# Attention and a gated layer on one core: the maxima's pieces spread anew over the groups, and an earlier load of the output weights

## The chip, the cores and the metric

The kernel runs on one core of a Trainium2 chip. The metric is the time of one execution on the device in microseconds. TensorE is PE in the profile (its weight loads PEld), VectorE is DVE, ScalarE ACT, GpSimd POOL, SyncE SP; here SP issues nearly all DMAs, into one queue.

## The reference

```python
x = L0_attn_x                          # 2 x 1024 x 512
xn = _layernorm(x)
s = attention(xn, w_qkv, b_qkv, w_out, b_out)      # 32 heads of 16, ALiBi slopes, causal
g = _silu(ffn(xn, w_gate, w_up, w_down))           # silu(gate) * up, then down; hidden 1360
x = x + s * g
```

The three matrices of `ffn` are built from octonion blocks of ternary weights: each weight is rounded to -1, 0 or 1 times the mean size. The scores get a bias per head and key (ALiBi) and the causal mask before the softmax.

## The kernel before, in words

**Stages.** (1) In four chunks of 512 tokens: layer norm, x turned on PE, queries, keys and values as three-term f16 products, stored to HBM. Inside the same stretch the weights are turned and split, and the octonion matrices of the gated layer are made. (2) The gated layer, again in four chunks; each has 26 tiles (`ffn(j, p)`): 22 gate and up tiles in turn (an even tile is a gate tile: ACT takes its tanh, then DVE multiplies; an odd one is multiplied by DVE at once) and 4 tiles of the down product. (3) Attention in 16 groups of four heads (2 batches of 8). (4) The output product, gate and residual, partly beside the last group.

**A group.** `scores(t, n, pair)` makes a tile of transposed scores with the mask added, 10 steps by 2 pairs; ACT takes the exponential; `products(t, n)` multiplies it with the values, 10 steps, with 32 columns of the array for each head. The exponential needs each row's maximum. So a pass goes ahead of the group: `fill_max(t, i)` (line 1519) computes scores once more, untransposed, into one of **three** PSUM banks, and DVE's `read_max` takes the maxima (line 1237 plain, line 1233 with the mask added). A group of heads has 42 such pieces: 41 tiles and, as piece 5, a transposition (line 1512) by which the maxima of the group before become two rows of its queries' operand (`Qs`, the name is `QKs` in the profile). Piece numbers 13 to 28 are plain 512-wide reduces; the others are masked, 128 to 512 wide. `fill_max` waits until DVE has read the piece three before it:

```python
elif at >= MRING:
    pe.wait_ge(max_read, tiles_read(at - MRING))
```

**The order of work.** `ORDER` is one list of all pieces of stages 2 to 4, written by `work_order`, and every engine walks through it. Beside stage 2 it strews the first pieces of the maxima (`early`: all 41 tiles of group 0 and pieces 0 to 18 of group 1) between the tiles of the third and fourth chunk: after each tile it computes how many are due and puts them in when that is at least three. In stage 3, one string `GROUP` of 72 letters (M a piece of the maxima, S scores, P products) gives the order within each group: 42 M, of which the first finish the next group's maxima and the last 14 or so begin those of the group after next. So each group begins with the same pieces done ahead.

**Loads.** `load(t)` on SP brings queries, keys, slopes and values of group t into one of three slots, with 15 DMAs; it is issued for t + 2 at the start of group t, once all scores of group t - 1 are filled. The first piece of group t + 2's maxima waits for all of them.

**The first stage's queue.** `store_qkv(c)` stores a query or key tile each time one is ready, with the loads of the gated layer's weights (`load_gated`, lines 512 to 523) between those of chunk 0; as number 6 the output weights (`w_out`, 1 MB, into `wslot[3]`, a part of `room`). Then come the four value stores. `next_x` (line 539) loads the next chunk's x. DVE's `third` and `values` write into two stage buffers each and wait for the store of the tile two before. `LN_AT[c][stage]` says after which query or key tile DVE does the five stages of the next chunk's layer norm (statistics, their sums, variance, root, normalising), `ROOT_AT[c]` when ACT takes the square root.

## Time and profile before

| | us |
|---|---|
| median of 3 runs | 829.93 |
| lowest, highest | 829.28, 832.33 |
| the profiled execution | 828.85 |
| its span | 827.0 |
| PE busy in the span | 794.2 (96%) |
| DVE busy | 606.6 (73%) |
| ACT busy | 473.6 (57%) |
| POOL busy | 172.0 (21%) |

The busy shares are means over the stages; the rows further down take the stages apart. The end of a matmul is modelled, and matmuls overlap in the array: two that use different halves of its rows run side by side. A row of the timeline gives the start, the busy time, and in brackets how long the engine idled before it and for whom.

### The profile page before, as it was taken

To read this page: it belongs to the slowest core of one execution; us is meant where nothing else is said; L and a number is where in the kernel's file an instruction comes from. 1 tells how busy PE (TensorE), PEld (TensorE's weight loads), DVE (VectorE), ACT (ScalarE), POOL (GpSimd) and SP (SyncE) were. 2 spreads that over 40 slices of the span, in tenths; PEclk is the share of its full clock that TensorE was granted. 3 is DMA by queue.
4 is the path that set the end of the run, shared out by engine and by line. 5 is a ranking of instruction groups with operands and counts; after the bars stand their busy time and mean duration, and the time that the engine had idled before them with its cause. 6 is when DMAs were issued, how large, how long until landed. Compare 5 with 4: busy or idle time off the path is not lost.

```text
span 827.0 us, 16157 instructions
## 1 busy us (share of the span) xinstructions
PE 794.2 (96%) x5927; PEld 350.2 (42%) x5927; DVE 606.6 (73%) x1743; ACT 473.6 (57%) x633; POOL 172.0 (21%) x214
## 2 busy tenths in 40 slices
PE   5989999999999999999999999999999999999998
PEld 3545444444444444444444434344343334343333
DVE  6837888643232464464599999999999999996546
ACT  7424384332232222232688888888888788887540
POOL 3223222233434333333300000000000003530000
PEclk9999999999999999999999999999999999999999
DMA  7474422259202101101222122222215233642736
GB/s 267 143 214 158 141 102 77 104 139 302 90 1 89 65 1 39 63 2 39 77 68 66 57 60 73 81 80 68 81 53 168 69 106 104 199 152 101 229 127 221
DMA packets 71104, 88.40 MB, mean 107 GB/s; under 512 B 26898, under 2 KB 37150, under 8 KB 70512
## 3 DMA queue, kind: packets, MB, share of 16 engines
q1 hardware_dynamic: 70992, 87.36, 32.8%
q8 instruction: 47, 0.77, 0.4%
q14 instruction: 33, 0.27, 0.1%
q0 software_dynamic: 32, 0.01, 0.0%
HBM read 51.15 MB, written 35.93 MB: 105 GB/s over the span
## 4 chain that ended last, share of the span: by engine, by line
PE 73%; DVE 15%; DMA 5%; issue 4%; ACT 1%; POOL 1%; SPq 0%; DVEq 0%; ACTq 0%
PE psum L1562 13%; PE psum L1519 9%; PE psum L1585 9%; PE psum L1586 9%; DVE mx L1237 9%; PE psum L1596 5%; PE psum L1597 5%; PE psum L1537 4%; DVE mshown L1233 3%; PE psum L1411 3%; PE psum L1413 3%; PE psum L1412 3%; PE psum L1546 2%; PE psum L1621 1%; PE psum L1623 1%
## 5 line engine op out<-in xcount | busy, mean ns | idle before, releaser
L951 ACT ACTIVATE probs<-psum,exp_scale 128x1024 f32<-128x1024 f32 (+1 forms) x320 | 310.2, 1028 | 66.2 <-PE psum L1546 46.3
L1233 DVE CUSTOM_DVE_ANT_0 mshown<-psum,ahead 128x384 bf16<-128x384 f32 (+3 forms) x512 | 220.2, 487 | 2.7 <-PE psum L1519 0.4
L1519 PE MATMUL psum<-QKs 51*128 51x512 f16 (+3 forms) x768 | 183.6, 332 | 12.6 <-DVE mx L1237 6.3
L1562 PE MATMUL psum<-probs,Vs 128*32 128x512 f32 (+3 forms) x1536 | 162.0, 510 | 0.2 <-ACT probs L951 0.2
L1237 DVE TENSOR_REDUCE mx<-psum 128x1 f32<-128x512 f32 x256 | 157.7, 681 | 3.5 <-PE psum L1519 2.5
L1537 PE MATMUL psum<-QKs 53*128 53x512 f16 (+3 forms) x768 | 138.1, 330 | 3.1 <-ACT probs L951 3.0
L1585 PE MATMUL psum<-X,room 128*128 128x512 f16 (+1 forms) x352 | 133.6, 380 | 0.0
L1586 PE MATMUL psum<-X,room 128*128 128x512 f16 (+1 forms) x352 | 133.4, 379 | 0.0
L1519 PEld LDWEIGHTS psum<-QKs 51*128 51x128 f16 x768 | 51.6, 93 | 146.8 <-DVE mx L1233 74.8
L983 ACT ACTIVATE room<-psum,gate_half 128x512 f32<-128x512 f32 (+1 forms) x44 | 30.2, 687 | 101.4 <-PE psum L1586 101.4
L1260 DVE SCALAR_TENSOR_TENSOR room<-room,psum 128x512 f32<-128x512 f32 (+1 forms) x44 | 30.2, 687 | 63.1 <-ACT room L983 63.1
L811 POOL TENSOR_TENSOR room<-room 128x512 f16<-128x512 f32 (+1 forms) x44 | 50.9, 1156 | 114.3 <-ACT room L988 114.3
L785 POOL TENSOR_SCALAR mscaled<-mx 128x32 f32<-128x32 f32 x16 | 4.6, 289 | 314.6 <-DVE mx L1245 314.6
L1596 PE MATMUL psum<-room 128*128 128x512 f16 (+1 forms) x176 | 66.8, 379 | 0.0
L1597 PE MATMUL psum<-room 128*128 128x512 f16 (+1 forms) x176 | 66.6, 379 | 0.0
L1562 PEld LDWEIGHTS psum<-probs,Vs 128*32 128x32 f32 x1536 | 44.8, 145 | 44.3 <-issue 37.7
L775 POOL TENSOR_TENSOR qk_stage<-rest,qk_stage 128x512 f16<-128x512 f32 x32 | 37.9, 1185 | 105.1 <-DVE qk_stage L1161 105.1
L1546 PE MATMUL psum<-unit,causal 64*128 64x64 bf16 (+1 forms) x768 | 58.8, 200 | 0.0
L1537 PEld LDWEIGHTS psum<-QKs 53*128 53x128 f16 x768 | 45.2, 94 | 23.7 <-ACT probs L951 12.0
L1546 PEld LDWEIGHTS psum<-unit,causal 64*128 64x128 bf16 x768 | 49.3, 96 | 13.1 <-issue 0.7
L1269 DVE SCALAR_TENSOR_TENSOR room<-room,psum 128x512 f32<-128x512 f32 x16 | 11.0, 687 | 58.9 <-ACT room L983 58.9
L1585 PEld LDWEIGHTS psum<-X,room 128*128 128x128 f16 (+1 forms) x352 | 35.0, 99 | 44.3 <-issue 5.3
(166 smaller groups left out, 963.0 us busy)
## 6 DMA issues: line engine op xcount, KB each, us to landing
o_scr<-osum SPq DMA_DIRECT2D x32, 256.0 KB, 3.1
QKs<-q_scr SPq DMA_DIRECT2D x96, 64.0 KB
QKs<-k_scr SPq DMA_DIRECT2D x96, 64.0 KB
q_scr<-qk_stage SPq DMA_DIRECT2D x16, 256.0 KB, 2.6
k_scr<-qk_stage SPq DMA_DIRECT2D x16, 256.0 KB, 2.2
v_scr<-v_stage SPq DMA_DIRECT2D x16, 256.0 KB, 2.1
Vs<-v_scr SPq DMA_DIRECT2D x16, 256.0 KB
probs<-in_L_attn_x SPq DMA_DIRECT2D x4, 1024.0 KB, 11.0
```

Of the source, the lines that this page charges most:

```text
L811: nc.gpsimd.tensor_tensor(HLs[0:n, t, :], hid[t % NSIG][0:n], HHs[0:n, t, :], ALU.subtract).then_inc(hl_done, 1)
L951: nc.scalar.activation(probs[n % PSLOTS][:, 2 * pair:2 * pair + 2, 0:COLS[n]], s_bank[pair][:, :, 0:COLS[n]], ACT.Exp, scale=exp_scale[:, ...
L1233: last = nc.vector.tensor_tensor_reduce(out=mshown[tiles_read(at) % 2][:, cols], in0=m_bank[bank][:, cols], in1=ahead[:, CH - keys:], scal ...
L1237: nc.vector.tensor_reduce(dst, m_bank[bank][:, 0:n * keys].rearrange("p (n k) -> p n k", n=n), AX.X, ALU.max).then_inc(max_read, 1)
L1519: last = nc.tensor.matmul(tile[:, hh, :], Qs[s][rows, pair + hh, qb * P:(qb + 1) * P], Ks[s][rows, pair + hh, k0:k0 + keys], start=(hh == ...
L1537: last = nc.tensor.matmul(s_bank[pair][:, u, at:at + cols], Ks[s][rows, pair, kb * P:(kb + 1) * P], Qs[s][rows, pair, (c + 1) * CH - cols: ...
L1546: last = nc.tensor.matmul(squares, causal[half, r], unit[half, 0, 0:HALF].unsqueeze(1).to_broadcast([HALF, len(blocks), HALF]), start=Fals ...
L1562: last = nc.tensor.matmul(pv_bank[32 * h:32 * h + 32, CH - cols:CH], Vs[s][:, kb, h::QH], probs[n % PSLOTS][:, h, at:at + cols], start=(kb ...
L1585: nc.tensor.matmul(bank[0:n], wt, X16[j % 2][:, 0, kt, :], start=(kt == 0), stop=False)
L1586: last = nc.tensor.matmul(bank[0:n], wt, X16[j % 2][:, 1, kt, :], start=False, stop=(kt == KT - 1))
L1596: nc.tensor.matmul(bank, HHs[0:n, k, tok], MD[0:n, k, :], start=(k == 0), stop=False)
L1597: last = nc.tensor.matmul(bank, HLs[0:n, k, tok], MD[0:n, k, :], start=False, stop=(k == HT - 1))
```

## The change

Three parts.

**The maxima run further ahead, and come back piece by piece.** `AHEAD` says how many pieces of the group after next's maxima are done when group t begins: 25 at group 0, one less with each group, 11 from group 14 on. So groups 1 to 13 hold 41 pieces, and 74 instead of 60 stand beside the gated layer (67 by `line(0)`, 8 more by `OPENING`, less the piece that group 0 doesn't need). They are strewn by the same rule as before (at least three due), which now gives batches of three and of four.

**Each group has its own string.** `GROUPS` has 15, by `GROUP_AT`; the last is the old one and serves groups 14 and 15. Group 0 has 33 pieces, and its first tile of scores is put at its very start.

**The output weights** are issued in the first queue, behind the bias row and ahead of the second chunk's x. The second chunk's layer norm moves by one tile, the root too.

```diff
+GROUPS = [
+    "SMSPPMPMSMMSMMSMSMPSMMMSPMSMMPS"
+    "MMSMPMMSMPMMSSMPMSMSMMPMSMSMSMSM",
+    "MPMSMPMMSMSPMMMSSMMPMSMMSMPMSMMSMPM"
+    "MSMSMPMMSMMSMMPMMSMPMSSMMMPMSMSMMSSM",
...
+GROUP_AT = [0, 1, 2, 3, 4, 5, 6, 7, 8, 9, 10, 11, 12, 13, 14, 14]
+PER_GROUP = 41
 OPENING = 8
-GROUP = "MPMMPSMMSMPMMSSMMMSSMMPMSMMSPMMSMPMM" \
-        "SMSMMPMSMMMMSSMPMMSPMMSSMMPMMSMSMMSM"
+AHEAD = [LEAD + (QUADS - 2 - t) * (NITEM - PER_GROUP) for t in range(QUADS - 1)] + [LEAD]
+
+
+def line(t):
+
+    return (t + 1) * NITEM + AHEAD[t]
...
-    items = [(t + 1, i) for i in range(LEAD, NITEM)] + [(t + 2, i) for i in range(LEAD)]
+    items = [divmod(i, NITEM) for i in range(line(t) + OPENING * (t == 0), line(t + 1) if t < QUADS - 1 else line(t) + NITEM)]
...
-    for kind in GROUP:
+    for kind in GROUPS[GROUP_AT[t]]:
...
-    early = [(0, i) for i in range(NITEM) if i != ROWS_AT] + [(1, i) for i in range(LEAD + OPENING)]
+    early = [divmod(i, NITEM) for i in range(line(0) + OPENING) if i != ROWS_AT]
...
         if t == 0:
-            opening = [w for w in pieces if w[0] == "maximum"][:OPENING]
-            pieces = [w for w in pieces if w not in opening]
+            pieces.sort(key=lambda w: w != ("scores", 0, 0, 0))
...
-        LN_AT = [[1, 2, 2, 3, 4], [2, 3, 4, 5, 6], [1, 2, 2, 3, 4]]
-        ROOT_AT = [2, 4, 2]
+        LN_AT = [[2, 3, 3, 4, 5], [2, 3, 4, 5, 6], [1, 2, 2, 3, 4]]
+        ROOT_AT = [3, 4, 2]
...
-                elif m == 6:
-                    sp.dma_start(wslot[3], w_out.rearrange("(t p) d -> p t d", p=P)).then_inc(w_loaded[3], 16)
...
             sp.dma_start(bv_row[:], b_qkv[2 * D:3 * D].partition_broadcast(P)).then_inc(bv_loaded, 16)
+            sp.dma_start(wslot[3], w_out.rearrange("(t p) d -> p t d", p=P)).then_inc(w_loaded[3], 16)
             next_x(1)
```

**SP, the first chunk.** Before: the start of the queue, then its part around the output weights (`room<-in_L_attn_w_out`); a name in brackets is the semaphore waited for.

```order
L595 DMA bv_row<-in_L_attn_b_qkv 128x512
L539 DMA xin<-in_L_attn_x 128x4x512 [waits xt_done]
...
L521 DMA room<-in_L_ffn_w_down 64x8x170
L529 DMA k_scr<-qk_stage 128x2x512 [waits q3_done]
L523 DMA room<-in_L_attn_w_out 128x4x512
L529 DMA k_scr<-qk_stage 128x2x512 [waits q3_done]
L535 DMA v_scr<-v_stage 128x512 [waits evac_done] x4
```

Now:

```order
L630 DMA bv_row<-in_L_attn_b_qkv 128x512
L631 DMA room<-in_L_attn_w_out 128x4x512
L574 DMA xin<-in_L_attn_x 128x4x512 [waits xt_done]
...
L558 DMA room<-in_L_ffn_w_down 64x8x170
L564 DMA k_scr<-qk_stage 128x2x512 [waits q3_done] x2
L570 DMA v_scr<-v_stage 128x512 [waits evac_done] x4
```

The output weights went from between the last two key stores to ahead of the second load of `xin`, and the value stores (`v_scr`) have only stores ahead of them.

**PE, the gated layer.** Before, a batch of the fourth chunk between two gate or up tiles; the lines 1585 and 1586 are a gate or up tile, line 1519 pieces of the maxima.

```order
L1586 MATMUL psum<-X,room 80x512
L1519 MATMUL psum<-QKs 128x512 [waits max_read] x3
L1585 MATMUL psum<-X,room 80x512 [waits f_evac]
L1586 MATMUL psum<-X,room 80x512
L1585 MATMUL psum<-X,room 80x512
```

Now a batch after tile 14 of the fourth chunk (lines 1621, 1622 and 1555 in the new file):

```order
L1622 MATMUL psum<-X,room 128x512
L1555 MATMUL psum<-QKs 128x512 [waits max_read] x4
L1621 MATMUL psum<-X,room 128x512 [waits f_evac]
L1622 MATMUL psum<-X,room 128x512
L1621 MATMUL psum<-X,room 128x512
```

Where every batch had three pieces, six of the 23 now have four; each piece waits for a bank (`max_read`).

**PE, the first group of attention.** Before (L1537 scores, L1546 their mask, L1519 pieces of the maxima), from the second tile of scores on:

```order
L1537 MATMUL psum<-QKs 128x512 [waits exp_done,f_evac]
L1537 MATMUL psum<-QKs 128x512
L1546 MATMUL psum<-unit,causal 128x64 x4
L1537 MATMUL psum<-QKs 128x256 [waits exp_done]
L1537 MATMUL psum<-QKs 128x256
L1546 MATMUL psum<-unit,causal 128x64 x4
L1537 MATMUL psum<-QKs 128x256 [waits exp_done]
L1537 MATMUL psum<-QKs 128x256
L1546 MATMUL psum<-unit,causal 128x64 x4
L1519 MATMUL psum<-QKs 128x512 [waits max_read] x3
```

Now, from the end of the gated layer (L1573 scores, L1582 mask, L1555 pieces):

```order
L1555 MATMUL psum<-QKs 128x128 [waits max_read] x2
L1555 MATMUL psum<-QKs 128x256 [waits max_read]
L1555 MATMUL psum<-QKs 128x256
L1573 MATMUL psum<-QKs 128x512 [waits exp_done,m_stacked,f_evac]
L1573 MATMUL psum<-QKs 128x512
L1582 MATMUL psum<-unit,causal 128x64 x4
L1555 MATMUL psum<-QKs 128x256 [waits max_read]
L1555 MATMUL psum<-QKs 128x256
L1573 MATMUL psum<-QKs 128x512 [waits exp_done,f_evac]
L1573 MATMUL psum<-QKs 128x512
L1582 MATMUL psum<-unit,causal 128x64 x4
L1555 MATMUL psum<-QKs 128x384 [waits max_read] x2
```

Four tiles of scores stood together ahead of the first piece; now pieces stand between the first and the second, and between all that follow.

## Rows read from the trace of the kernel before

**Rows 1.** Stage windows: us; per engine busy (instructions); granted clock, DMA share, GB/s.
```profile
56.32:279.70 223.38, 223.27 (x1146) 106.09 (x1148) 118.19 (x242) 86.96 (x163) 74.26 (x62) 1.00 0.37 122
279.70:400.00 120.30, 120.30 (x575) 51.14 (x576) 64.15 (x165) 31.11 (x51) 43.90 (x39) 1.00 0.08 31
...
401.36:755.00 353.64, 339.74 (x3502) 140.51 (x3506) 347.00 (x1181) 300.29 (x337) 36.34 (x68) 0.99 0.31 91
```

**Rows 2.** Waits of the whole run: waiting line <- awaited line: us, times, longest.
```profile
PEld psum L1519 <- DVE mx L1233: 74.8, 153, 0.8
```

**Rows 3.** Window of one group of four heads.
```profile
448.06:471.98 23.92, 23.12 (x245) 9.57 (x246) 23.59 (x80) 20.47 (x23) 0.74 (x3) 1.00 0.24 67
```

**Rows 4.** Timeline, PE, 30 to 57 us: start, us, instruction, [idle before it <- releaser].
```profile
32.80 0.66 PE L1380 MATMUL psum<-identf,room 128*128 128x128 f32 x4 [0.89 <-DVE W L1065]
...
56.32 0.39 PE L1411 MATMUL psum<-X,W 128*128 128x512 f16 x1 [2.35 <-DVE X L1057]
```

**Rows 5.** Timeline, SyncE's DMA issues, 15 to 60 us.
```profile
15.21 0.37 SPq L539 DMA_DIRECT2D xin<-in_L_attn_x  x1
...
45.19 0.47 SPq L523 DMA_DIRECT2D room<-in_L_attn_w_out  x1
...
47.65 9.95 SPq L535 DMA_DIRECT2D v_scr<-v_stage  x4
```

**Rows 6.** Timeline, DVE, 15 to 60 us.
```profile
29.04 2.47 DVE L1029 BATCH_NORM_STATS2 stats<-xin 128x6 f32<-128x512 f32 x4
31.66 0.43 DVE L1161 CAST qk_stage<-rest 128x512 f16<-128x512 f32 x1
...
54.69 1.06 DVE L1166 TENSOR_TENSOR v_stage<-psum,bvs_row 128x512 f32<-128x512 f32 x1 [4.97 <-DMA v_scr<-v_stage]
```

**Rows 7.** DMA issues up to 90 us: what, count, KB each, median us to landing.
```profile
room<-in_L_attn_w_out SPq DMA_DIRECT2D x1, 1024.0 KB, 6.6
```

**Rows 8.** Timeline, PE, 296 to 304 us: around a batch of three maxima.
```profile
298.99 0.38 PE L1586 MATMUL psum<-X,room 128*128 128x512 f16 x1
...
299.83 0.39 PE L1585 MATMUL psum<-X,room 128*128 128x512 f16 x1
```

**Rows 9.** Timeline, DVE, in one group: sixteen plain reduces, one narrow masked one.
```profile
448.63 9.91 DVE L1237 TENSOR_REDUCE mx<-psum 128x1 f32<-128x512 f32 x16
458.45 0.28 DVE L1233 CUSTOM_DVE_ANT_0 mshown<-psum,ahead 128x128 bf16<-128x128 f32 x1
```

**Rows 10.** Timeline, DVE, gated layer: odd tile at 305.23, even at 311.77.
```profile
305.23 0.69 DVE L1256 SCALAR_TENSOR_TENSOR room<-psum,room 128x512 f32<-128x512 f32 x1 [0.32 <-PE psum L1586]
305.83 1.87 DVE L1237 TENSOR_REDUCE mx<-psum 128x1 f32<-128x512 f32 x3
...
311.77 0.69 DVE L1260 SCALAR_TENSOR_TENSOR room<-room,psum 128x512 f32<-128x512 f32 x1 [1.75 <-ACT room L983]
312.37 1.88 DVE L1237 TENSOR_REDUCE mx<-psum 128x1 f32<-128x512 f32 x3
```

**Rows 11.** Timeline, ACT, gated layer: the tanh of the same even tile.
```profile
311.05 0.69 ACT L983 ACTIVATE room<-psum,gate_half 128x512 f32<-128x512 f32 x1 [2.25 <-PE psum L1586]
```

**Rows 12.** Timeline, PE, one step of products.
```profile
459.75 1.09 PE L1562 MATMUL psum<-probs,Vs 128*32 128x512 f32 x8
```

**Rows 13.** Timeline, SyncE: first and last issue of a group's 15 loads.
```profile
446.12 0.79 SPq L553 DMA_DIRECT2D QKs<-q_scr  x2
...
452.59 0.52 SPq L561 DMA_DIRECT2D Vs<-v_scr  x1
```

**Rows 14.** Windows of 2 us: clock and DMA share.
```profile
54.00:56.00 2.00, 0.00 (x0) 0.00 (x0) 1.31 (x2) 0.00 (x0) 0.00 (x0) 1.00 0.02 9
400.00:402.00 2.00, 1.09 (x15) 0.56 (x15) 1.25 (x3) 1.84 (x3) 0.41 (x1) 1.00 0.34 131
404.00:406.00 2.00, 2.00 (x19) 1.25 (x15) 2.00 (x4) 1.19 (x2) 0.20 (x1) 0.50 0.37 134
456.00:458.00 2.00, 2.00 (x21) 0.78 (x24) 2.00 (x5) 2.00 (x3) 0.00 (x0) 1.00 0.03 8
```

More of the change, by code:

```diff
@@ L154, in tiles_read @@
     return at + 1 - rows_copied(at)
+GROUPS = [
[3 more added lines that the diff above has]
+    "MSMSMPMMSMMSMMPMMSMPMSSMMMPMSMSMMSSM",
+    "MPMSMMSPMSMMPMSMMSMMPMSMMSMPMMSSMMP"
+    "MMSMSMPMMSMSMMPMMMSPMMSMSMPMSMSMMSSM",
+    "MPMSMMSMPMSMPMMSMSMMMPMSMSMMPMSMMSP"
+    "MSMMSMMPMMSMSMMPMMSMSPMMSMPMMSMSSMSM",
+    "MPMSMPMMSSMMMSMPMMSMMSMPMMSMSMPMSMM"
+    "SMPMMSSMMPMMSMSMMPMMSMSMPMMSMSPMMSSM",
+    "MPMMSMSPMMMSMSMPMMSMSMMMPSMMSMPMSMM"
+    "SMPMMSMSMPMMSMSMMPMSMMSMPSMMMSPMSMMS",
+    "MPMSMSMPMSMMSMMSSMMPMMSMMSMPMSMPMSM"
+    "MPMSSMMPMSMMPMMSMMSMMSMMPMMSSMPMMSMS",
+    "MPMSMMMSPMSMMSMSSMMMPMSMMSMMPMSMPMM"
+    "SMPMSMSMPMSMMPMMSMSMMPMSMMPMSSMMMSMS",
+    "MPMSMSMMSMMMSSMSMMPSMMPMMSMSMMPMMPM"
+    "SMSMMPMSSMMPMMSMPMMSSMMMPMMSMSPMMSSM",
+    "MPMMSSMMPMSMSMSMMSMMSMSMPMMSMSMMPMS"
+    "MPMMSMPMMSSMPMSMMPMMSMSMMPMMMSPMMSSM",
+    "MPMSMSMMPSMMSMSMSMMMSMSMMPMMSMMSMPM"
+    "SMPMSMMPMMSMSPMMSMPMMSMSMMPMSMSMPMSM",
+    "MPMMSSMMMPSMMMSMSSMMPMSMSMMPMSMMSMM"
+    "MSMPMMSMPMSMSMPMSMMPMMSSMMMPSMMPSMSM",
+    "MPMSMSMPMMSMPMSMMSMPMSMSMPMSMMPMMSM"
+    "MSMPMMSSMMPMSMMSMPMMSSMMPMMSMMSMMSSM",
+    "MPMMSSMMPMSMPMSSMMMPMMSMSPMSMMPMSMM"
+    "MSMMPSMSMMPMSMMMSPMMSSMMPMMSMSMMSMSM",
+    "MPMMPSMMSMPMMSSMMMSSMMPMSMMSPMMSMPMM"
+    "SMSMMPMSMMMMSSMPMMSPMMSSMMPMMSMSMMSM",
+]
+GROUP_AT = [0, 1, 2, 3, 4, 5, 6, 7, 8, 9, 10, 11, 12, 13, 14, 14]
+PER_GROUP = 41
 OPENING = 8
-GROUP = "MPMMPSMMSMPMMSSMMMSSMMPMSMMSPMMSMPMM" \
-        "SMSMMPMSMMMMSSMPMMSPMMSSMMPMMSMSMMSM"
+AHEAD = [LEAD + (QUADS - 2 - t) * (NITEM - PER_GROUP) for t in range(QUADS - 1)] + [LEAD]
+def line(t):
+    return (t + 1) * NITEM + AHEAD[t]
 def group_order(t):
     scores = [(n, pair) for n in range(NST) for pair in range(2)]
-    items = [(t + 1, i) for i in range(LEAD, NITEM)] + [(t + 2, i) for i in range(LEAD)]
+    items = [divmod(i, NITEM) for i in range(line(t) + OPENING * (t == 0), line(t + 1) if t < QUADS - 1 else line(t) + NITEM)]
     products = [(t - 1, n) for n in range(NST - LAG, NST)] + [(t, n) for n in range(NST - LAG)]
     out = []
-    for kind in GROUP:
+    for kind in GROUPS[GROUP_AT[t]]:
         if kind == "S":
```

## Prediction

> **What bounds the kernel now.** I read the stage windows first: three stages and a tail. Up to 280 us and on to 400 us the tensor engine is busy all the time [rows 1]; that is where every microsecond of its work or idleness goes straight into the end. From 401.36 to 755 us DVE is busy 347.00 of 353.64 us [rows 1], and the page's waits show what that does to the tensor engine: its weight loads for the maxima wait 74.8 us in all for the masked reads of line 1233 alone [rows 2]. One group in this stage takes 23.92 us, of which DVE is busy 23.59, ACT 20.47 [rows 3]; the matmul column reads 23.12, but modelled ends hide short stops, and I take the tensor engine to have some 3 to 4 us of room a group. So the group stage is DVE's: shorten what DVE reads there and the stage shrinks, as long as the pieces can go where DVE has room. The gated stage has that room (DVE 64.15 of 120.30 us) but none on the tensor engine. After 755 us nothing changes. The rest of the idleness lies before 57 us: the tensor engine stops 2.35 us before the second chunk's first matmul and 0.89 us before a weight transposition [rows 4].
>
> Sum and rows are made against the profiled execution, 828.85 us (span 827.0), which stands 1.08 us under the median of 829.93.
>
> **1. Output weights earlier, layer norm one tile later.** Now the last 1 MB of weights is issued at 45.19 us, just ahead of the last key store and of the four value stores, issued from 47.65 us [rows 5]. DVE cannot write its third value tile before the first value store has landed: it idles 4.97 us and starts at 54.69 [rows 6], the split of x queued behind it ends after that, and the tensor engine's 2.35 us follow. With the weights gone from there the stores have 1 MB less ahead of them. DVE would have been free 4.97 us earlier, twice what the tensor engine waited, so the 2.35 us go wholly; next in line is the third value tile itself, which the tensor engine finishes before its last one. The weights now come between the projection weights and x of the second chunk, issued at 15.21 us and first read at 29.04 [rows 5, 6]: 13.8 us of slack against 6.6 us in which those weights landed in the busy place [rows 7]. That costs nothing. The 0.89 us come from DVE taking x's statistics (2.47 us at 29.04) ahead of the copy at 31.66 that lets the low weights go on [rows 4, 6]. Now the statistics stand one tile later. But each copy also needs an earlier store to have landed, and the normalising of x moves nearer to its transpositions at 44 us, so I take back about half: 0.5. Bounds: -3.2 us (both stops gone) and 0 (the stop only moves). I take **-2.9**.
>
> **2. Fourteen more pieces beside the gated layer, as matmuls.** There were 60 pieces (20 batches of three); the order now has 74 in 23 batches: one of two, sixteen of three, six of four. A batch of three 512-wide pieces takes the tensor engine from the slot after 298.99 (a slot there is 0.216 us, 299.205) to 299.83, so 0.62 us [rows 8], 0.21 a piece. Fourteen make 2.9, some of them narrow: **+2.7** (bounds 1.5, if the fourth of a batch runs beside the third on the other half of the rows, and 3.5).
>
> **3. The batches of four.** The maxima have three PSUM banks. The fourth piece of a batch fills the bank of the first, which DVE must have read; the tensor engine waits in order with the whole gated layer behind it. Never so before: all batches had three. How long it waits is in the trace. After an even gate tile (ends as ACT begins at 311.05) DVE first waits for the tanh, multiplies at 311.77 and reads its first maximum at 312.37; the read takes 0.62 us (16 in 9.91 us [rows 9]), so the bank is free 1.94 us after the tile's end [rows 10, 11]. The three fills take until about 0.36 us after it. The stop is 1.6 us. After an odd tile DVE multiplies at once (305.23) and reads at 305.83: free 1.22 us after the tile's end, a stop of 0.9 [rows 10]. Three of the six follow even tiles (14 of the third chunk, 2 and 14 of the fourth), three follow odd ones (21 of the third, 7 and 21 of the fourth): 3 x 1.6 + 3 x 0.9 = **+7.5**. The tensor engine has no other idle place to absorb it. Bounds: 4 (the next batch is already queued and DVE is early) and 9.
>
> **4. What DVE no longer reads after 401.36.** The pieces read after the last gated tile began with number 16 of the second group, now with number 30: numbers 16 to 28 are plain reduces, 13 x 0.62 = 8.06 us; number 29 is two masked 128-wide reads of 0.28 us that overlap a little [rows 9], about 0.45. **-8.5**. Each group after the first then has 41 pieces where it had 42, and lasts about 23.3 us instead of 23.92. ACT (20.47) still fits under that, and so does the tensor engine.
>
> **5. The orders by group.** The cover is now thinner: three engines between 88% (20.47 of 23.3) and 99%, three banks, and products that hold the tensor engine for 1.09 us [rows 12], in which three narrow pieces (0.28 us each) run out. DVE idles 6.6 us in the whole stage before the change. A different order in every group could save a tenth of a microsecond a group or lose three tenths. I take **+1.0** (bounds -2 and +4). The loads of the group after next must also land earlier, because its first piece comes after some 16 of the next group's instead of 28. They are issued from 446.12 to 452.59 us and the DMA engines are quiet from 456 on [rows 13, 14]: under 10 us; its first piece in the second group is filled about 9 to 10 us after the same point. So at most half a microsecond, once, and later groups have more. The number is in the +1.0.
>
> Sum: -2.9 + 2.7 + 7.5 - 8.5 + 1.0 = -0.2. 828.65 for the profiled execution, about 829.7 for the median; I say **829.5 us**. About 0.5% (4.1 us) is what a measurement of this kernel can tell from no change.
>
> **Rivals.**
> - *The stops of the fours don't come.* If DVE has always read the first bank when the fourth fill is due, part 3 is 1 to 3 us and the sum -5 to -7: 823 to 825. For it: DVE is busy only half of that stage. Against it: the reads start where the rows say, behind the tanh, and nothing can move them forward. With a group stage that comes out well (part 5 at -2) it also passes the 0.5%. Chance for faster on all such grounds 0.27.
> - *The clock falls at the new stops.* In the window 400 to 402 us the tensor engine was busy 1.09 of 2 us, and from 404 to 406 the granted clock is 0.50, the 1.2 GHz level instead of 2.4 [rows 14]. If that follows each of the six stops, then every time some 4 us of matmuls run at half speed in a stage that the tensor engine bounds: 2 us each, up to +12, so 834 to 842, slower. It decides as soon as three of the six do it. Against it: from 54 to 56 us the engine did nothing at all and the clock stayed at 1.00 [rows 14]; the two falls of the trace lie in the group stage, where matmuls use half the rows or 32 columns. The Trainium skill, "TensorE: Matmul & The Clock Gate", section "A second HAM failure mode: psum-queue depth-cycling", has it that short idle stops while PSUM banks are cycled can be enough to make the clock swing; by that rule this rival would be the likeliest and the time near 840. The trace agrees in the group stage and not at 54 us. Chance 0.13.
> - *The group stage loses its cover.* If each of fourteen groups idles 0.4 us more than now, part 5 is +6 and the time 835: slower. It is the point at which tensor engine work, not DVE reads, sets the group. Chance 0.10.
> - *The load does nothing.* If the value stores are slow for another reason than the weights, part 1 is 0 and the time 832.5: within 0.5%.
>
> **How the numbers follow.** Neutral 0.50, faster 0.27, slower 0.23 (the two slower rivals). The two parts that move most, 3 and 4, nearly cancel, and each is sized from rows; the neutral case's own range is 826 to 833. The overall range reaches to the favourable end of part 3 and to two or three clock falls or a loose group stage: 824 to 836.
>
> **What would show it.** The tensor engine busy without a stop from about 15 to 279 us except the small ones at the start, no wait at the second chunk; the value tile's wait for its store gone. In the gated stage (longer by 10 us, DVE busy some 8 us more) six new waits of the fills for DVE, 1.6 or 0.9 us. Read after that: 14 groups of about 23.3 us, DVE at 98%. Wrong would be: a gated stage longer by 3 us only (faster), granted clock under 1.00 in it (slower), groups still at 23.9 us (slower), or a wait for the loads at the start of the second group's pieces for the fourth.

## The result, and the profile after

| us | before | after |
|---|---|---|
| median (4 runs each) | 829.61 | 840.95 |
| lowest, highest | 826.9, 832.33 | 837.07, 842.26 |
| ratio to before | | 1.0134 (1.0106 to 1.0161) |
| the profiled execution, its span | 828.85, 827.0 | 839.78, 838.0 |

The changed kernel is slower by 1.3%, 11.3 us. I had forecast no change (829.5, range 824 to 836): wrong, and outside the range.

**Where the 11 us are.** The stage windows of the changed kernel stand against [rows 1]. To have the same borders in both kernels I cut at three events: the first gate tile, the first scores, and the last join of the partial maxima (`whole_rows`). In each row: its length; PE, PEld, DVE, ACT and POOL busy, with the number of instructions; granted clock, DMA share, GB/s. Before:

```profile
160.40:400.20 239.80, 239.80 (x1132) 105.77 (x1131) 102.80 (x221) 66.05 (x107) 89.59 (x77) 1.00 0.23 76
400.20:755.49 355.29, 341.12 (x3521) 141.13 (x3517) 348.06 (x1183) 301.82 (x339) 36.34 (x68) 0.99 0.31 92
```

After:

```profile
159.10:413.30 254.20, 246.68 (x1145) 107.06 (x1144) 111.48 (x238) 65.93 (x107) 89.67 (x77) 0.99 0.21 72
413.30:766.82 353.52, 339.52 (x3506) 138.19 (x3502) 339.86 (x1166) 303.36 (x339) 36.37 (x68) 0.99 0.32 92
```

Up to the first gate tile 1.3 us are gained (160.40 to 159.10), in the gated stage 14.4 are lost (239.80 to 254.20), in the group stage 1.8 gained (355.29 to 353.52), and the tail gains 0.3 (71.51 to 71.18): together 11.0 of span. Both DVE numbers of the group stage matter: its busy time fell by 8.2 us (348.06 to 339.86), and its idle time rose by 6.4 (7.23 to 13.66).

**Gated stage: six stops.** The timeline of PE has these idle times in the gated layer of the changed kernel, and no others; line 1555 is the old 1519:

```profile
304.62 0.39 PE L1555 MATMUL psum<-QKs 51*128 51x512 f16 x1 [1.57 <-DVE mx L1273]
...
321.54 0.23 PE L1555 MATMUL psum<-QKs 51*128 51x128 f16 x1 [1.00 <-DVE mx L1273]
```

```profile
349.30 0.39 PE L1555 MATMUL psum<-QKs 51*128 51x512 f16 x1 [1.58 <-DVE mx L1269]
...
360.43 0.33 PE L1555 MATMUL psum<-QKs 51*128 51x384 f16 x1 [0.96 <-DVE mx L1269]
...
376.29 0.39 PE L1555 MATMUL psum<-QKs 51*128 51x512 f16 x1 [1.57 <-DVE mx L1273]
```

```profile
393.21 0.39 PE L1555 MATMUL psum<-QKs 51*128 51x512 f16 x1 [0.84 <-DVE mx L1273]
```

That is 1.57 + 1.00 + 1.58 + 0.96 + 1.57 + 0.84 = 7.52 us, which is what PE idles by the window (254.20 - 246.68). They are the fourth pieces of the six batches. DVE's timeline has the reason at the first of them: it multiplies behind the tanh at 303.27, and the four reads start at 303.88.

```profile
303.27 0.69 DVE L1296 SCALAR_TENSOR_TENSOR room<-room,psum 128x512 f32<-128x512 f32 x1 [1.75 <-ACT room L1019]
303.88 2.48 DVE L1273 TENSOR_REDUCE mx<-psum 128x1 f32<-128x512 f32 x4
```

**The clock.** Windows of the changed kernel around the first stop, the second, the fourth and fifth, and at the opening of the group stage:

```profile
300.00:320.00 20.00, 18.43 (x78) 7.35 (x76) 11.81 (x19) 5.12 (x9) 4.86 (x5) 0.91 0.00 0
320.00:340.00 20.00, 19.00 (x93) 8.34 (x93) 6.09 (x23) 2.69 (x4) 8.74 (x8) 1.00 0.17 66
360.00:380.00 20.00, 18.00 (x76) 6.99 (x77) 11.98 (x31) 4.82 (x8) 4.62 (x4) 0.92 0.00 1
418.00:424.00 6.00, 6.00 (x42) 2.46 (x45) 4.06 (x20) 3.63 (x5) 0.75 (x3) 0.50 0.12 45
```

From 300 to 320 us the mean granted clock is 0.91, from 360 to 380 it is 0.92: twice the engine went to the 1.2 GHz level for a while in stretches with a stop (not in that of the second, 320 to 340 us, nor behind the other three stops). Before the change this stage had no fall: [rows 1] shows a clock of 1.00 up to 400 us. A mean of 0.91 over 20 us is 1.8 us of full-speed work lost (20 x 0.09), 0.92 is 1.6. From 418 to 424 it was at 1.2 GHz throughout, at the start of the group stage, and a product took 1.94 us instead of the 1.09 of [rows 12]:

```profile
420.28 1.94 PE L1598 MATMUL psum<-probs,Vs 128*32 128x512 f32 x8
...
427.30 1.09 PE L1598 MATMUL psum<-probs,Vs 128*32 128x512 f32 x8
```

**Group stage.** The windows of some groups of the changed kernel, cut at the second `osum` copy of each group (as the 23.92 us of [rows 3]; there DVE idled 0.3):

```profile
441.82:465.40 23.58, 23.10 (x243) 9.24 (x242) 23.26 (x80) 20.39 (x24) 0.75 (x3) 1.00 0.25 74
465.40:488.85 23.45, 22.82 (x244) 9.23 (x242) 23.00 (x79) 20.42 (x24) 0.75 (x3) 1.00 0.25 72
488.85:513.46 24.61, 23.84 (x253) 9.75 (x251) 24.04 (x85) 21.25 (x24) 0.75 (x3) 1.00 0.25 72
537.11:562.08 24.97, 24.50 (x263) 10.24 (x259) 24.37 (x87) 22.56 (x25) 0.75 (x3) 1.00 0.24 71
634.20:662.27 28.07, 24.70 (x244) 9.56 (x241) 25.32 (x84) 20.80 (x25) 0.75 (x3) 0.94 0.45 139
662.27:684.40 22.13, 21.64 (x236) 8.90 (x233) 21.47 (x76) 18.73 (x22) 0.75 (x3) 1.00 0.29 81
684.40:705.83 21.43, 20.43 (x216) 8.17 (x214) 20.07 (x76) 17.98 (x21) 0.75 (x3) 1.00 0.34 98
```

A group is no longer one length. The first two are 23.58 and 23.45, others 24.6 and 25.0, two late ones 22.1 and 21.4: with 41 pieces from a ring of 42, a string holds other widths each time (DVE has 76 to 87 instructions in them). DVE's idle time is 0.3 to 0.7 us in most, 1.36 in the one from 684.40, and 2.75 in the one from 634.20, where the denominators are turned into reciprocals.

These windows hold different amounts of reading. Windows from one join to the next always hold 42 pieces, and DVE's work in them stays nearly the same. Here is one of before and the worst ordinary one of after:

```profile
683.65:707.55 23.90, 23.11 (x249) 9.56 (x241) 23.64 (x81) 20.46 (x24) 7.44 (x10) 1.00 0.36 112
```

```profile
693.74:718.83 25.09, 24.82 (x261) 9.87 (x257) 23.81 (x82) 21.16 (x24) 6.90 (x9) 1.00 0.61 149
```

DVE idles 0.26 us in the first and 1.28 in the second. The first join comes 9.5 us earlier behind the start of the stage than before (7.82 us for 17.35), which is the work that was taken away; the fourteen intervals that follow take 345.70 us instead of 337.94, and that is where it goes. Of these 7.8 us the first interval has 3.1 (26.99 for 23.91), the one with the reciprocals 1.5 (28.15 for 26.67), the two behind it 1.8 (24.74 and 25.09 for 24.17 and 23.90), and the other ten together 1.4.

The first group and the reciprocals' one before, and the first one after, for comparison:

```profile
400.20:427.10 26.90, 24.96 (x258) 10.91 (x256) 24.83 (x83) 22.62 (x25) 3.27 (x5) 0.94 0.19 62
642.36:669.03 26.67, 25.12 (x245) 10.54 (x247) 25.26 (x84) 20.58 (x25) 0.74 (x3) 0.94 0.24 70
```

```profile
413.30:441.82 28.52, 26.27 (x263) 10.99 (x261) 24.40 (x83) 23.51 (x26) 3.28 (x5) 0.88 0.17 57
```

DVE idled 2.07 us in the first group and idles 4.12 now; with the reciprocals it idled 1.41.

**A DMA wait with the reciprocals.** In that group PE has a stop that the kernel before hasn't. It waits for two stores of 8 KB that bring the rows of maxima (`mrows`) into the queries' operand:

```profile
652.83 0.39 PE L1573 MATMUL psum<-QKs 53*128 53x512 f16 x2 [2.74 <-DMA QKs<-mrows]
```

SP's queue, after and then before, has eight loads of 256 KB each (`sums_room`) ahead of them:

```profile
635.83 4.96 SPq L675 DMA_DIRECT2D sums_room<-o_scr  x8
...
643.83 1.38 SPq L603 DMA_DIRECT2D QKs<-mrows  x2
```

```profile
621.97 5.07 SPq L639 DMA_DIRECT2D sums_room<-o_scr  x8
...
636.04 1.41 SPq L568 DMA_DIRECT2D QKs<-mrows  x2
```

The small stores are now issued 8.0 us behind the start of these loads, where it was 14.1 us, and PE wants them 6.3 us after their issue, at 650.09. No other group has such a wait. No experiment moves the stores, so that the loads cause it is read from the queue and not shown by a run; the distance alone doesn't decide, since in experiment 8 it is 6.1 us and PE doesn't wait.

**The first stage.** Of the two stops of [rows 4] the long one is gone, the short one stays at its place:

```profile
33.87 0.66 PE L1416 MATMUL psum<-identf,room 128*128 128x128 f32 x4 [0.86 <-DVE W L1101]
```

### The profile page after: what moved, and what is told of

It reads as the page before. It is cut to its first block, busy times and chain, and to the rows that moved or that the text cites. A ratio compares the mean times of both kernels' runs of the same rounds, so it can differ in the third digit from the quotient of the medians.

```text
span 838.0 us, 16156 instructions
## 1 busy us (share of the span) xinstructions
PE 800.8 (96%) x5927; PEld 349.8 (42%) x5927; DVE 606.9 (72%) x1743; ACT 475.1 (57%) x633; POOL 172.2 (21%) x214
## 4 chain that ended last, share of the span: by engine, by line
PE 81%; DVE 10%; issue 4%; DMA 2%; ACT 2%; SPq 0%; POOL 0%; DVEq 0%; ACTq 0%
PE psum L1598 15%; PE psum L1555 11%; PE psum L1621 9%; PE psum L1622 9%; DVE mx L1273 6%; PE psum L1573 5%; PE psum L1632 5%; PE psum L1633 5%; PE psum L1447 3%; PE psum L1449 3%; PE psum L1448 3%; DVE mshown L1269 2%; PE psum L1657 2%; PE psum L1659 2%; PE psum L1461 2%
## 5 line engine op out<-in xcount | busy, mean ns | idle before, releaser
L1555 PE MATMUL psum<-QKs 51*128 51x512 f16 (+3 forms) x768 | 183.2, 332 | 16.7 <-DVE mx L1273 8.2
L1573 PE MATMUL psum<-QKs 53*128 53x512 f16 (+3 forms) x768 | 139.9, 331 | 6.4 <-ACT probs L987 2.8
L1621 PE MATMUL psum<-X,room 128*128 128x512 f16 (+1 forms) x352 | 135.6, 385 | 0.0
L1622 PE MATMUL psum<-X,room 128*128 128x512 f16 (+1 forms) x352 | 135.4, 385 | 0.0
L1555 PEld LDWEIGHTS psum<-QKs 51*128 51x128 f16 x768 | 53.9, 94 | 150.3 <-DVE mx L1269 77.7
L1582 PE MATMUL psum<-unit,causal 64*128 64x64 bf16 (+1 forms) x768 | 62.6, 199 | 0.0
L1573 PEld LDWEIGHTS psum<-QKs 53*128 53x128 f16 x768 | 41.0, 94 | 35.2 <-ACT probs L987 22.3
L1582 PEld LDWEIGHTS psum<-unit,causal 64*128 64x128 bf16 x768 | 47.6, 96 | 16.0 <-issue 1.1
```

The costliest lines, as they stand in the source:

```text
L1555: last = nc.tensor.matmul(tile[:, hh, :], Qs[s][rows, pair + hh, qb * P:(qb + 1) * P], Ks[s][rows, pair + hh, k0:k0 + keys], start=(hh == ...
L1573: last = nc.tensor.matmul(s_bank[pair][:, u, at:at + cols], Ks[s][rows, pair, kb * P:(kb + 1) * P], Qs[s][rows, pair, (c + 1) * CH - cols: ...
L1582: last = nc.tensor.matmul(squares, causal[half, r], unit[half, 0, 0:HALF].unsqueeze(1).to_broadcast([HALF, len(blocks), HALF]), start=Fals ...
L1621: nc.tensor.matmul(bank[0:n], wt, X16[j % 2][:, 0, kt, :], start=(kt == 0), stop=False)
L1622: last = nc.tensor.matmul(bank[0:n], wt, X16[j % 2][:, 1, kt, :], start=False, stop=(kt == KT - 1))
```

## The experiments

Each stands against runs of the kernel before on the same chip (medians 828.70 to 829.54). Stage lengths are of the profiled execution: gated from the first gate tile to the first scores, groups from there to the last join.

### 1. Batches of at most three

```diff
         if due - given >= (MRING if given else len(early) % MRING or MRING):
+            due = min(due, given + MRING)
             order += [("maximum", *x) for x in early[given:due]]
```

The changed kernel, with its 74 early pieces in 25 batches.

> The changed kernel, with the 74 early pieces put in three at a time (25 batches, none of four); the order of the groups is untouched. My theory: the six stops of 0.84 to 1.58 us (7.5 us in the trace of the change) and the two stretches of half clock behind them (3.4 us each, 1.7 us lost each) are 11 us of the 14.7 us by which the gated stage grew. So the six stops vanish, the clock stays at 1.00 between 276 and 400 us, and the time falls by 10 to 11 us, to 830 +- 2. Rival (the fourteen pieces themselves cost the time, the stops only show where): the gated stage keeps more than 8 of its 14.7 us and the time stays above 836.

Measured: 827.54 us (10 runs), ratio 0.9981 (0.9959 to 1.0003), so 13.4 under the changed kernel, just below the 828 to 832 that I expected, and not distinct from before.

```profile
158.90:401.20 242.30, 242.30 (x1146) 105.77 (x1145) 111.31 (x238) 65.93 (x107) 89.68 (x77) 1.00 0.24 75
401.20:754.42 353.22, 340.08 (x3506) 138.70 (x3502) 340.07 (x1165) 303.55 (x339) 36.40 (x68) 0.98 0.33 92
```

The gated stage has no idle time, no fall of the clock, and takes 242.30 us: 2.5 more than before, and those are the fourteen pieces. Against the changed kernel it is 11.9 shorter, of which 7.5 are the stops. The batches of four are the whole loss against the kernel before. The group stage stays at 353.22 with 13.15 us of DVE idle, so what it fails to win has nothing to do with the stops.

### 2. The kernel before with batches of four

```diff
-        if due - given >= (MRING if given else len(early) % MRING or MRING):
+        if due - given >= MRING + 1:
+            due = given + MRING + 1
```

> The kernel before, its 60 early pieces put in four at a time (15 batches of four instead of 20 of three). Theory: 15 stops, 8 behind a tanh at 1.57 us and 7 behind an odd tile at 0.94 us, 19 us, less 5 changes of operand at 0.2 us: 18 us more in the gated stage, and for each third stop a stretch of half clock (1.7 us): 5 more, 8 us. So 847 to 858. Rival (DVE or the gated layer absorbs most of a stop once the first have passed): under 840.

Measured: 856.01 us, ratio 1.0324 (1.0283 to 1.0364). The 60 pieces are the old ones, only in fifteen batches of four.

```profile
160.40:428.10 267.70, 248.95 (x1131) 108.43 (x1130) 104.97 (x223) 66.60 (x107) 90.34 (x78) 0.97 0.20 69
```

The stage takes 27.9 us more. PE idles 267.70 - 248.95 = 18.75 us, 1.25 a batch, and its busy time has grown by 9.15 us. The windows of the stage show four falls of the clock for the fifteen stops: means of 0.83 over 10 us from 300, and of 0.91 over 20 us from 335, 370 and 400, about 7 us of full-speed work in all, and 1.00 everywhere else in the stage. An estimate for the rest: a matmul behind a stop shows 0.39 us, where one in a full stream takes a slot of 0.216 (the prediction's number), so each stop breaks up about 0.17 us of overlap, 2.6 us for fifteen. So the clock goes along with some of the stops: about 0.5 us to a batch here, 3.4 for six in the changed kernel. The time lies in the expected 847 to 858.

### 3. Early weights and shifted layer norm in the kernel before

```diff
-        LN_AT = [[1, 2, 2, 3, 4], [2, 3, 4, 5, 6], [1, 2, 2, 3, 4]]
-        ROOT_AT = [2, 4, 2]
+        LN_AT = [[2, 3, 3, 4, 5], [2, 3, 4, 5, 6], [1, 2, 2, 3, 4]]
+        ROOT_AT = [3, 4, 2]
...
-                elif m == 6:
-                    sp.dma_start(wslot[3], w_out.rearrange("(t p) d -> p t d", p=P)).then_inc(w_loaded[3], 16)
...
+            sp.dma_start(wslot[3], w_out.rearrange("(t p) d -> p t d", p=P)).then_inc(w_loaded[3], 16)
             next_x(1)
```

> The kernel before with only the early load of the output weights and the layer norm one tile later. From the trace of the change: the 2.35 us stop is gone, the 0.9 us stop stays, so 2.3 us less than before: 827.3. Rival (the earlier load brings on the half clock of 3.4 us near 15 us that the trace of the change has and the one of before has not): such a stretch shows again, costs 1.1 us, and the gain is 1.2 us or less.

Measured: 826.51 us (10 runs), ratio 0.9963 (0.9944 to 0.9982), 0.8 below what I had expected. The second chunk's stop has gone; the one at the third weight transposition has not. The rival's half clock near 15 us isn't there either; of the other traces with the early load only that of experiment 9 has one, so the load doesn't bring it on each time. PE, then DVE, from 25 to 60 us of this kernel:

```profile
33.23 0.66 PE L1379 MATMUL psum<-identf,room 128*128 128x128 f32 x4 [0.86 <-DVE W L1064]
```

```profile
32.09 0.43 DVE L1160 CAST qk_stage<-rest 128x512 f16<-128x512 f32 x1 [2.62 <-DMA q_scr<-qk_stage]
...
51.81 1.08 DVE L1165 TENSOR_TENSOR v_stage<-psum,bvs_row 128x512 f32<-128x512 f32 x1 [1.53 <-DMA v_scr<-v_stage]
```

The cast at 32.09 waits 2.62 us for a store of `q_scr`, with the statistics out of its way; the copy that PE waits for is queued behind it. The value tile's wait, 4.97 us in [rows 6], is 1.53.

### 4. Early weights alone

The same without the two lines on `LN_AT` and `ROOT_AT`.

> Base: the kernel of before with the output weights loaded early; here the layer norm of the second chunk stands where it stood before the change (statistics in tile 1, not 2), so the only edit to the kernel before is the place of one load. Theory (the stop of 2.35 us came from the weights alone; the shift of the layer norm moved nothing, since the copy that it was to free waits for the first query store to land): time as with both, 826.5, within 1 us. Rival (the shift carries a part of the gain): 827.0 to 827.8, and a stop of about 0.9 us at tile 3 that is longer than with both.

Measured: 826.36 us (10 runs), ratio 0.9957 (0.9936 to 0.9978): the same as with both. The first gate tile is at 157.80 us (160.40 before), and PE's stop:

```profile
32.83 0.66 PE L1379 MATMUL psum<-identf,room 128*128 128x128 f32 x4 [0.84 <-DVE W L1064]
```

0.84 us against 0.86 with the shift. All of the gain that the runs can tell is the place of one load; the shift added nothing to it.

### 5. The store of x behind three query stores

```diff
-                if c < 2:
+                if c == 1:
                     sp.wait_ge(xl_done, c * KT + KT)
                     sp.dma_start(x_scr[c], ...)
...
+                    if c == 0 and m == 2:
+                        sp.wait_ge(xl_done, KT)
+                        sp.dma_start(x_scr[0], ...)
```

On top of experiment 3, in `store_qkv`; the 1 MB store of x stood ahead of the first query store.

> Base: early weights and the shifted layer norm; here the 1 MB store of the first chunk's x is issued behind the first three query stores instead of ahead of them. Theory (the stop of 0.86 us at tile 3 stays because the DVE copy behind it waits for the first query store, which lies behind 1 MB of x): the wait of 2.62 us of DVE for q_scr goes, the tensor engine's stop goes, time 825.7, 0.9 less than the base. Rival (the copy is late for DVE's own work, or another store takes its place): the stop stays or moves by a tile, time 826.5.

Measured: 828.55 us (12 runs), ratio 0.9989 (0.9971 to 1.0006); by the medians 2 us slower than its base, and 2.2 slower than experiment 4 on the same chip. The stop at the third weight transposition went, and another took its place at the first value tile, behind which the clock fell (matmuls of 0.63 us for 0.38):

```profile
43.57 0.39 PE L1425 MATMUL psum<-W,X 128*128 128x512 f16 x1 [2.10 <-DVE W L1067]
...
45.15 0.63 PE L1427 MATMUL psum<-W,X 128*128 128x512 f16 x1
```

```profile
31.13 0.43 DVE L1163 CAST qk_stage<-rest 128x512 f16<-128x512 f32 x1 [1.34 <-DMA q_scr<-qk_stage]
...
42.43 0.43 DVE L1163 CAST qk_stage<-rest 128x512 f16<-128x512 f32 x1 [3.32 <-DMA q_scr<-qk_stage]
```

DVE's cast now waits 3.32 us at 42.43 for the store behind the megabyte. The rival had the mechanism: a store took the other's place, and the copy of the last weights, queued behind that cast, holds PE for 2.10 us instead of 0.86. Its time, 826.5, was too low. Later places of that megabyte weren't tried.

### 6. Four tiles of scores first, as before

```diff
-            pieces.sort(key=lambda w: w != ("scores", 0, 0, 0))
+            pieces.sort(key=lambda w: not (w[0] == "scores" and w[2] < 2))
```

The changed kernel, its opening of the first group only.

> The changed kernel, with the first four tiles of scores (two steps, two pairs) put ahead of the first group's pieces as before the change. In the change the second tile of scores stands behind a piece that waits 1.11 us for DVE, the clock then falls for 6.8 us instead of 3.4, and the first group's maxima take 27.0 us where they took 23.9. Theory: the mixed opening makes this; now one stretch of 3.4 us at most and 2 to 3 us less: 838 to 839. Rival (the stops of the gated layer or the group's own string make it): the first group stays at 27 us, no difference to 841.

Measured: 838.75 us, ratio 1.0106 (1.0065 to 1.0148). That is the time I expected, by luck: its interval overlaps that of the changed kernel, and what was to save the time didn't happen. The low clock at the start of the group stage stays (6.8 us of it in the trace, as in the changed kernel), and from the first join to the second it takes 27.05 us, against 26.99: the mixed opening isn't the cause. The gated stage gave something else:

```profile
158.20:409.10 250.90, 243.37 (x1148) 106.32 (x1147) 111.53 (x238) 65.97 (x107) 89.65 (x77) 1.00 0.21 73
```

The same six stops (7.53 us) with the clock at 1.00: they don't bring it down every time. Without a fall six batches of four still cost 250.90 - 242.30 = 8.6 us, 1.1 beyond the idle time (the estimate of experiment 2, 0.17 us a stop, gives 1.0), and the changed kernel's two falls another 3.3.

This trace also says something about the groups, since its strings are those of the changed kernel. From the second join on, the intervals agree with the changed kernel's to 0.02 us, but for the one with the reciprocals: 26.64 us here, 28.15 there. PE's wait for `mrows` in it is 1.90 us here, 2.74 there, and DVE idles 1.20 us for 2.71. So what that group loses isn't fixed by its string.

### 7. One string for groups 1 to 13

```diff
-    for kind in GROUPS[GROUP_AT[t]]:
+    for kind in GROUPS[GROUP_AT[t]] if t in (0, 14, 15) else GROUPS[14].replace("MMMM", "MMM"):
```

On top of experiment 1, as are the next three.

> Batches of three (e1), with one string for the groups 1 to 13: the old one with one M of its row of four left out. Theory (the strings of their own don't make the loss; what makes it is that 41 pieces shift their widths against any string, where the old string was fitted to one phase): the 42-piece intervals are as uneven as e1's or worse, 24.2 to 25.5 us, and the time is 0 to 8 us over e1. Rival (the own strings are the loss): intervals of 23.9 us or less, 3 us faster than e1.

Measured: 847.91 us, ratio 1.0228 (1.0199 to 1.0257): 20.4 above experiment 1, far past what I had expected. One group, in which the old string has met other widths:

```profile
479.24:504.69 25.45, 23.66 (x242) 9.16 (x240) 23.50 (x81) 20.33 (x25) 0.74 (x3) 1.00 0.22 66
```

DVE works 23.50 us in it, no more than in [rows 3], and idles 1.95. From join to join such groups take 25.64 to 26.38 us, where the kernel before has 23.9.

### 8. The old string, shifted by fourteen pieces

```diff
-LEAD = 11
+LEAD = 25
...
-PER_GROUP = 41
+PER_GROUP = 42
...
-    for kind in GROUPS[GROUP_AT[t]]:
+    for kind in GROUPS[14] if t else GROUPS[14].replace("M", "", OPENING):
```

Now every group has all 42 pieces in the old order; only the maxima run fourteen pieces further ahead, all the time.

> 25 pieces ahead in every group and 42 a group with the old string (the first group with eight M fewer), batches of three. Nothing is taken from a group but the last one; the widths stand 14 pieces further in the string than it was fitted to. Theory: the 42-piece intervals are longer than the 23.91 us of before by 0.3 us or more, only by the phase; and the pieces saved come back in the last group that has any, by up to 8 us there. Rival (phase means nothing): 23.9 us intervals. If the loads of the group after next come too late, the fill of the first piece waits for them in each group, where the change could show it only in the second.

Measured: 857.69 us, ratio 1.036 (1.032 to 1.040). Each group takes 25.62 us, as regular as the 23.92 before, with nearly the same work for DVE. From join to join DVE has 81 or 82 instructions in both kernels, busy 23.83 us here and 23.64 before:

```profile
480.51:506.13 25.62, 23.83 (x244) 9.28 (x241) 23.83 (x82) 20.64 (x24) 0.74 (x3) 1.00 0.22 65
```

DVE idles 1.79 us where it idled 0.33. The rival, loads that come too late, isn't it: the fills wait for a load in 5 places of the stage, 2.7 us of PEld's time in all, and not once in this group. What is left is order. The 7 us or so that I expected back at the end don't show: the first join comes 7.5 us earlier than before, but behind the last one the kernel needs 78.87 us instead of 71.51. DVE's idle times and PE's work in part of this group:

```profile
484.37 0.69 DVE L1270 CUSTOM_DVE_ANT_0 mshown<-psum,ahead 128x512 bf16<-128x512 f32 x1 [0.30 <-PE psum L1556]
...
491.21 0.56 DVE L1270 CUSTOM_DVE_ANT_0 mshown<-psum,ahead 128x384 bf16<-128x384 f32 x1 [0.72 <-PE psum L1556]
...
496.31 8.72 DVE L1274 TENSOR_REDUCE mx<-psum 128x1 f32<-128x512 f32 x14 [0.34 <-PE psum L1556]
```

```profile
488.85 0.26 PE L1549 MATMUL psum<-ident,mparts 128*96 128x128 f16 x1 [0.16 <-DVE mx L1270]
489.54 0.33 PE L1556 MATMUL psum<-QKs 51*128 51x384 f16 x1 [0.43 <-DVE mx L1270]
489.81 1.09 PE L1599 MATMUL psum<-probs,Vs 128*32 128x512 f32 x8
490.84 0.33 PE L1556 MATMUL psum<-QKs 51*128 51x384 f16 x1
```

At 489.54 PE gets a bank, fills it with a piece 384 wide, and takes a product from 489.81 to 490.90. The next fill starts at 490.84 and ends at 491.17. When the product began DVE had one read of 384 under way and one left, was through at 490.48, and starts again at 491.21, after 0.72 us. A 384-wide read takes 0.56 us and a 512-wide one 0.69, so what stands in the banks when a product of 1.09 us begins decides whether DVE lasts through it, and the phase of the string against the widths sets that. I have followed it at this one place; that the other idle times of the group come the same way is an inference.

### 9. The old string in the first group

```diff
+    for kind in GROUPS[GROUP_AT[t]] if t else GROUPS[14].replace("M", "", 9):
```

> Batches of three (e1), with the old string for the first group, less its first nine M. In e1 the first 42 pieces after the gated layer take 26.75 us against 23.9 before; the clock is at half for 6.8 us then, and a product of 1.94 us at half clock stands ahead of the next fills with one piece left in the banks (1.81 us of DVE idle). Theory: the first group's own string makes that; with three or more 512-wide pieces ahead of each early product the interval falls to 24 to 25 us and the time by 1.5 to 2.5 us. Rival (the half clock alone makes it): it stays above 26.

Measured: 828.33 us (10 runs), ratio 0.9992 (0.9967 to 1.0017), within noise of experiment 1. In the profiled execution the clock didn't fall in this group, and from the first join to the second it took 24.67 us (26.75 in experiment 1), but a later one was 1.1 longer (25.80 for 24.73), with a fall of its own. The interval came out as the theory had it, but the fall of the clock, which the rival wanted as the cause, was missing too, so this doesn't tell the string from the clock. In the medians the first group's own string is worth nothing that the runs can tell.

### 10. Without the mask

```diff
-                                     ACT.Exp, scale=exp_scale[:, 0:1]).then_inc(exp_done, 1)
+                                     ACT.Exp, scale=1.0e-12).then_inc(exp_done, 1)
...
-                if n in DIAG:
+                if False:
```

> Batches of three (e1) without the 48 small mask matmuls of each group, and with a constant scale in the exponential so that it stays finite: the scores have no causal mask. Theory: in the changed kernel's middle groups DVE idles 0.2 to 0.6 us more than before over 42 pieces, because fills come late behind TensorE's other work. The mask matmuls take TensorE some 1.8 us a group, so without them the 42 pieces from whole rows to whole rows take 23.6 to 23.8 us in every group, 24.73 and 25.08 of e1 among them. Rival (the order of letters alone sets the idle time, each product of 1.09 us with too few pieces in the banks ahead of it): the intervals stay within 0.1 us of those of e1.

This kernel leaves out the mask's matmuls and takes a constant scale in the exponential. Measured: 830.71 us, a single run. Two windows of 20 us, the first in a group with the clock full, the second where it fell:

```profile
480.00:500.00 20.00, 19.12 (x164) 5.72 (x156) 19.50 (x60) 16.31 (x20) 0.74 (x3) 1.00 0.19 53
580.00:600.00 20.00, 18.86 (x139) 5.90 (x134) 17.66 (x56) 14.48 (x19) 0.74 (x3) 0.86 0.20 57
```

In the nine intervals between joins in which the clock was full, this kernel differs from experiment 1 by -0.32 to +0.25 us: 24.06 for 23.81 and 23.97 for 23.97 at the start, 24.45 for 24.73 and 24.76 for 25.08 late, where DVE idles most (0.96 and 1.27 us in experiment 1). Neither the 23.6 to 23.8 of the theory nor the rival's 0.1 holds: less work for PE takes some 0.3 us off the two late ones and nothing clear off the others. The clock over the whole group stage was 0.96 where experiment 1 has 0.98, and the run isn't faster. It shows that PE's room isn't the large part, and no more.

## Why the prediction was wrong, step by step

**What bounds the kernel.** Right for the first two stages. For the third it was half the truth: "DVE's" holds only as long as the order keeps DVE fed. Experiment 8 has DVE with nearly the same work (23.83 us for 23.64 from join to join), the same counts and 25.62 us a group.

**1. Weights and layer norm (-2.9).** Measured: -2.6 at the first gate tile in experiment 4, -3.2 in the medians; -1.3 in the changed kernel's profile, which had a fall of the clock in its first 20 us. The 2.35 us came out whole, as said. The half of the 0.89 that I took was wrong (0.84 and 0.86 stay with and without the shift), for the reason that I had named and priced at half: the earlier store. The trace of before had it, though not in the rows that I showed: SP issues the 1 MB store of x at 25.87 us and the first query store behind it at 27.63.

**2. Fourteen pieces (+2.7).** Measured 2.5 (experiment 1).

**3. Batches of four (+7.5).** Measured 7.52 of idle time, each stop within 0.1 of its size: 1.57, 1.58, 1.57 for 1.6 and 1.00, 0.96, 0.84 for 0.9. The whole price was more: 8.6 with a full clock (experiment 6), the difference most likely the overlap that each stop breaks up, and 11.9 with two falls.

**The clock rival (0.13).** It asked for three falls in six; the profile has two. The time, 840.95, lies in its range and for a mixture of reasons: 3.3 us are the clock's. The Trainium skill, "TensorE: Matmul & The Clock Gate", section "A second HAM failure mode: psum-queue depth-cycling", has short idle stops as enough for a swing; the traces agree part of the time: two of six stops (changed kernel), none of the same six (experiment 6), and four falls for fifteen stops, a clock of 0.97 over the stage (experiment 2). My argument against it, one stop of 2.35 us without a fall, was one draw from such a lot, and worth far less than I gave for it.

**4. What DVE no longer reads (-8.5).** Measured: DVE is busy 8.2 us less in the group stage. The term was right as work.

**5. The strings (+1.0, bounds -2 and +4): the step that failed.** DVE idles 13.66 us where it idled 7.23: +6.4, outside the bounds. The windows give three parts.

- 3.0 us are spread over the ordinary groups. This part is the order: the traces of the changed kernel and of experiments 1 and 6, which have the same strings, repeat it to 0.02 us in every interval. It is a quarter of a microsecond a group in the mean, but half of it lies in the two intervals behind the reciprocals.
- 2.05 us are in the first group (4.12 for 2.07; the clock's mean there is 0.88 for 0.94). String and clock aren't told apart here.
- 1.3 us are in the group with the reciprocals (2.75 for 1.41). The string doesn't fix it: the same one gave 1.20 us of idle time between its joins in experiment 6 and 2.71 in the changed kernel. PE's new wait for `mrows`, 1.90 and 2.74 us, goes along with it; my sum had no term for that.

I had named the mechanism of the first part, products of 1.09 us in which narrow pieces run out, and sized it between a tenth of a microsecond won and three tenths lost a group, with no row behind either, and took +1.0. The loads for the group after next, priced in the same term, cost one weight load 0.3 us in the changed kernel. What I could have read from the trace: only 0.33 us of DVE idle time stand in a group of before, so that order had little left to win and much to lose, and each shift leaves its phase. Experiments 7 and 8 give the price of the old string out of phase, 1.7 to 2.5 us a group; fifteen strings of their own avoid most of that, but not the last 0.3. The rival "the group stage loses its cover" (0.4 a group, +6, chance 0.10) came out right in size and not in its reason: PE's work was to set the group, and experiment 10 shows that this is at most a small part.

**The sum.** With measured terms: -1.3 (weights, clock at the start in), +2.5, +7.5, +4.4 (clock and broken overlap at the stops), -8.2, +6.4, -0.3 (tail) = +11.0, the difference of the spans. Terms 4 and 5 were to give 7.5 and gave 1.8, and the clock took 3 to 4 that the sum had at nothing. Only one of the two, with all else as forecast, would have left the time in its range: 829.5 + 5.7 = 835.2, or 829.5 + 4 = 833.5. Experiment 1 checks the rest of the sum without the fours: it should have gained 7.7 us and gained 1.5 (827.54 for 829.08), so most of the 6.2 that are missing are the group stage's.

**Open.** Why a stop sometimes brings the clock down and mostly doesn't: the same order of the gated layer did both, in the changed kernel and in experiment 6. Whether strings exist that hold 41 pieces with 0.3 us of DVE idle time a group; no other set was tried. How much of the first group's loss is its string and how much the clock. What the wait for `mrows` costs by itself: 1.90 us of it went with an interval as short as before (26.64, experiment 6), 2.74 with 28.15, and the two small stores weren't put ahead of the eight loads in any run.

**The better version.** Experiment 4: the kernel before with one load moved, 826.36 us, 0.4% under before and 1.7% under the change (826.36 / 840.95 = 0.9826).

## What to carry to other kernels

A batch that is longer than its ring of banks makes an in-order engine wait for the reader within the batch: each time by as much as the reader starts late, readable from the trace beforehand; cap the batch at the ring, which here costs nothing that the runs can tell and gives 13 us. Work taken off the engine that bounds a stage can come back as its idle time, here 6.4 us of 8.2, unless the order still feeds it: price a changed phase from experiments, not by the small idle time of the order that it leaves. And where one queue feeds several waits, look for the largest transfer ahead of each wait, and ask whether the change moves a small transfer closer behind it.

## What the runs showed of the hardware

- The clock's falls vary between executions with the same stops: six stops of 0.84 to 1.58 us in a busy stage came with a stage clock of 0.99 (changed kernel) and of 1.00 (experiment 6).
- A stop costs more than its idle time: 8.6 us for 7.53, at a clock of 1.00 (experiment 6 against experiment 1).
- Less work on PE didn't keep the clock up in the one execution without the mask's matmuls: 0.96 over the group stage with 2806 matmul records, 0.98 with 3506 in experiment 1. With a spread like that of the first point, one execution doesn't show that it lowers the clock.
- Two stores of 8 KB issued 8.0 us behind the start of eight 256 KB loads in one queue kept PE waiting for 2.74 us (changed kernel) and 1.90 us (experiment 6); in groups without those loads the same stores kept it waiting nowhere.
- The same instructions in the same string, fourteen pieces out of phase, cost 1.7 us in 23.9 (experiment 8): 7% of a group from order alone.
